# A full-array product ahead of each score tile in a two-layer transformer kernel

## What is computed

```python
x = x + _L0_xattn_ref(_layernorm(x), ctx_512, ...)   # 16 heads of 8: causal self attention + attention to ctx
x = x + _L0_ffn_ref(_layernorm(x), ...)              # 8 experts 128 -> 512 -> 128, weighted by the top 2
x = x + _L1_xattn_ref(_layernorm(x), ctx_512, ctx_512, ...)  # one head of 128
x = x + _L1_ffn_ref(_layernorm(x), ...)              # 16 heads of 64, values and outputs chosen by gates
...
att = jnp.where(causal, jnp.einsum('bhqd,bhkd->bhqk', q, k) * scale, -jnp.inf)
y = jnp.einsum('bhqk,bhkd->bhqd', jax.nn.softmax(att, axis=-1), v)
```

## Time and profile before

| | |
|---|---|
| median of 3 runs | 1716.87 us (1716.63 to 1721.53) |
| the profiled execution's own time | 1711.72 us |
| its span, first to last instruction | 1710.0 us |
| mean granted TensorE clock over the span | 0.718 of 2.4 GHz |
| TensorE busy | 1310.1 us (77%) |
| VectorE busy | 718.0 us (42%) |
| ScalarE busy | 488.1 us (29%) |

### The profile page before, as it was taken

How to read it: one execution, slowest core, us unless ns; L and a number is a source line. 1 busy time by engine, 2 the same in 40 slices (tenths; PEclk the granted TensorE clock), 3 DMA queues, 4 the chain that set the end, 5 groups by cost and what they waited for, 6 DMA issues and landing times.

```text
span 1710.0 us, 21323 instructions
## 1 busy us (share of the span) xinstructions
PE 1310.1 (77%) x8530; PEld 1008.1 (59%) x8530; DVE 718.0 (42%) x1958; ACT 488.1 (29%) x1003; POOL 77.1 (5%) x134
## 2 busy tenths in 40 slices
PE   2777668887679777896788777897688876897566
PEld 2446545775458654685457654596457754586366
DVE  2623492335822385225813376214832349122700
ACT  0233314224133232333143232333132231332120
POOL 0010001000010000100010000100010000100000
PEclk9657766787667875697658875697666976677655
DMA  5000010311012110301103110301103101121131
GB/s 157 7 1 4 0 31 4 64 44 26 12 28 43 38 28 10 64 19 28 34 1 64 44 29 10 58 13 41 25 10 64 44 16 22 26 41 38 37 59 46
DMA packets 197498, 56.85 MB, mean 33 GB/s; under 512 B 173029, under 2 KB 193303, under 8 KB 197399
## 3 DMA queue, kind: packets, MB, share of 16 engines
q1 hardware_dynamic: 195318, 51.30, 14.2%
q10 hardware_dynamic: 2080, 4.19, 0.8%
HBM read 31.36 MB, written 24.12 MB: 32 GB/s over the span
## 4 chain that ended last, share of the span: by engine, by line
PE 60%; DVE 23%; ACT 7%; issue 4%; DMA 3%; SPq 0%; ACTq 0%; DVEq 0%
PE bank L942 8%; PE bank L766 8%; PE bank L792 7%; DVE negmax L1179 6%; PE bank L692 6%; PE bank L904 4%; PE bank L618 4%; ACT pa L1012 3%; DVE negc L1331 3%; PE bank L925 3%; PE bank L707 2%; DVE qk_lo L1323 2%; DMA at<-at_d 2%; PE bank L956 2%; PE bank L717 2%
## 5 line engine op out<-in xcount | busy, mean ns | idle before, releaser
L1012 ACT ACTIVATE pa<-bank 128x512 f32<-128x512 f32 x224 | 123.4, 597 | 351.5 <-PE bank L707 266.2
L942 PE MATMUL bank<-vb,pb 128*128 128x65 f32 x1024 | 147.2, 315 | 12.2 <-issue 12.2
L942 PEld LDWEIGHTS bank<-vb,pb 128*128 128x128 f32 x1024 | 145.8, 232 | 16.4 <-issue 16.3
L766 PE MATMUL bank<-xnT_a,w 128*128 128x256 f32 x512 | 145.9, 436 | 0.0
L1179 DVE TENSOR_REDUCE negmax<-bank 128x2 f32<-128x512 f32 (+1 forms) x224 | 138.8, 682 | 16.2 <-PE bank L653 11.6
L1029 ACT ACTIVATE pa<-bank,b_c 128x256 f32<-128x256 f32 x256 | 107.3, 470 | 127.8 <-PE bank L766 126.4
L792 PEld LDWEIGHTS bank<-w,pa 128*128 128x128 f32 x1024 | 124.1, 193 | 3.0
L792 PE MATMUL bank<-w,pa 128*128 128x128 f32 x1024 | 124.1, 276 | 0.0
L766 PEld LDWEIGHTS bank<-xnT_a,w 128*128 128x128 f32 x512 | 106.7, 219 | 21.9 <-issue 7.0
L1087 ACT ACTIVATE pb<-bank 128x512 f32<-128x512 f32 x128 | 69.5, 595 | 169.7 <-PE bank L908 169.4
L692 PE MATMUL bank<-pa,va 128*32 128x256 f32 (+1 forms) x1024 | 101.8, 550 | 16.4 <-ACT pa L1012 15.9
(11 more groups left out here) (231 smaller groups left out, 1972.3 us busy)
## 6 DMA issues: line engine op xcount, KB each, us to landing
v_d<-vb SPq DMA_DIRECT2D x16, 512.0 KB, 5.1
vb<-v_d SPq DMA_DIRECT2D x16, 512.0 KB, 5.7
at_d<-at SPq DMA_DIRECT2D x32, 256.0 KB, 2.1
at<-at_d SPq DMA_DIRECT2D x32, 256.0 KB, 4.3
pv_d<-pvs SPq DMA_DIRECT2D x8, 512.0 KB, 2.8
pvs<-pv_d SPq DMA_DIRECT2D x16, 256.0 KB, 4.3
w<-in_L_ffn_W_dram ACTq DMA_DIRECT2D x1, 2048.0 KB, 10.4
bd<-mix_d SPq DMA_DIRECT2D x128, 8.0 KB
```

Source lines behind the costliest of these rows:

```text
L766: mm = pe.matmul(BA[u % 2][:, c * T:(c + 1) * T], w1[:, e, f:f + P], xnT_a[:, :], start=True, stop=True)
L942: mm = pe.matmul(BB[2 + qt][:, i * (DH + 1):(i + 1) * (DH + 1)], pb[:, h % NPB, kt * T + qt * P:kt * T + (qt + 1) * P], vb[:, kt, h, :], s ...
L1012: nc.scalar.activation(pa[:, e % NPA, :], BA[e % 2][:, :], ACT.Exp, scale=SC0).then_inc(S["a_ex"], 1)
```

## The change

A helper makes one product of the full array: `ident_b` (128x128 bf16) as weights and `mask_qk`, repeated four times, as 512 columns. It writes a whole bank. It is called after the wait for the bank and ahead of the bank's first score product, whose `start=True` lets the scores overwrite it. In `a_max` it is called for the four banks of blocks 1 to 6, in `a_score` for the two banks of pairs 1 to 13, in `b_max` for both banks of all eight blocks, in `b_score` for both banks of pairs 1 to 7.

```diff
+                    def full_array(bank):
+
+                        pe.matmul(bank[:, :].rearrange("p (n k) -> p n k", n=4), ident_b[:, :],
+                                  mask_qk[:, :].unsqueeze(1).broadcast_to([P, 4, P]), start=True, stop=True)
...
                                     if g == 0:
                                         pe.wait_ge(S["a_mx"], upto("a_mx", 4 * m - 3 + j))
+                                        full_array(BA[j])
                                     pe.matmul(BA[j][:, g * P:(g + 1) * P], qs[strips[j], sc, g, 0:P], ks[strips[j], sc, g, 0:P],
                                               start=(g == 0), stop=True, skip_group_check=True)
...
                                 if m > 0 and c == 0:
                                     pe.wait_ge(S["a_mx"], upto("a_mx", 4 * m - 3 + j))
+                                    full_array(BA[j])
...
                                     if n > 0 and kt == 0:
                                         pe.wait_ge(S["a_ex"], upto("a_ex", 2 * n - 1 + i))
+                                        full_array(BA[i])
...
                                     if c == 0:
                                         pe.wait_ge(S["a_ex"], upto("a_ex", 2 * n - 1 + i))
+                                        full_array(BA[i])
...
                                     if g == 0:
                                         pe.wait_ge(S["a_ex"], upto("a_ex", 2 * n - 1 + i))
+                                        full_array(BA[i])
...
                                 rows = slice(64 * j, 64 * j + 64)
+                                if c == 0:
+                                    full_array(BB[(2 * m + j + 2) % 4])
...
                                     if pr > 0 and kt == 0 and part == 0:
                                         pe.wait_ge(S["b_ex"], upto("b_ex", 2 * pr - 1 + i))
+                                        full_array(BB[i])
```

## The result

The changed kernel takes 1881.4 us (median of four runs, 1879.9 to 1898.4), the kernel before beside it 1719.1 (four runs): ratio 1.097, 95% interval 1.091 to 1.103, or +162 us. Forecast were 1949 us and +232, range 1770 to 2090. Some executions of a kernel are slower as a whole, at a lower granted clock: ratios and intervals leave them out, medians keep them.

The account below looks back on a forecast made before the run. It saw TensorE busy 77% of the span, mostly near half clock in partial-array stretches, with VectorE bounding the second maxima stretch. Seven periods at +27 (+189) plus ends +43 gave +232, 1949 us; range 1770 to 2090.

Parts of the forecast that it names:

- Price of one: Each added product in line, stream plus entering and leaving the strips: 0.94 us at half clock, 0.6 at full clock.
- Maxima, +13: Both attentions' maxima, per period: products in line, partly under VectorE's work, lengthen them by 13 us (4 to 26).
- First scores, +8: First attention's scores, per period: longer pairs, partly repaid by faster value products, +8 us (-1.5 to +21).
- I take six of these hot: First attention's scores: six of eight value-product heads per period reach full clock, 0.95 instead of 1.91 us each, -5.7 us.
- its clock 0.6 to 0.8: Sign of being right: the first-score stretch, 658 to 704, grows by some 8 us with its clock at this level.
- Second scores, +6: Second attention's scores beside the expert layers, per period: five pairs, two products each, +6 us (5 to 7).
- First period, +23 of the ends: First period, without second attention: six maxima blocks add 15 us and the scores 8.
- End, +20: End of the kernel, 1604 to 1704, at clock 0.50 throughout: score pairs add 14 us and maxima 6.
- seven score pairs x 2.1 = +14: End of the kernel: each of seven second-attention score pairs grows by 2.1 us at clock 0.50, +14 us.
- The clock wins all over: Rival: products raise the clock in maxima and scores and it holds; +8 us per period, 1783 us; chance 0.14.
- It never rises: Rival: the clock stays down, all products cost 0.94 us plus strips; 2148 us; chance 0.06.
- Faster: Rival: waits hide half the products, full clock in first scores takes off 14 us per period; 1673 us; chance 0.09.

Follow-up runs that it names:

- the winner: Two full-array products ahead of each first-attention score pair's wait (pairs 1 to 13), in a free bank, added to the kernel before, no others: 1664.4 us, ratio 0.973.

## Why the prediction was right, and where it was off

**Sign and mechanism: right.** Slower (0.88) came, inside the range; +162 against a forecast of +232 (0.70 of it; 0.80 by the profiled executions, 187). That the product costs more in line than its clock wins is shown by the runs: with the borders gathered the same 640 products cost +27, and 26 per sequence ahead of the wait turn the sign. The size is in part luck, since terms missed in both directions: the first scores more than forecast, the maxima, second scores and end less.

**Price of one.** Forecast 0.94 cold and 0.6 hot. Measured 1.05 - 0.21 = 0.84 cold: the borders are 0.41 together, not 0.51. They are counted from load to load here and from stream to stream in the forecast, so only the sum compares. At full clock, from the timeline of after:

```profile
1421.41 0.39 PE L598 MATMUL bank<-mask_qk,ident_b 128*128 128x512 bf16 x1 [0.78 <-ACT pa L1025]
...
1421.73 0.32 PE L736 MATMUL bank<-qs,ks 32*128 32x128 f32 x1
...
1421.98 0.39 PE L598 MATMUL bank<-mask_qk,ident_b 128*128 128x512 bf16 x1
```

0.32 + 0.25 = 0.57 for a product and a strip of 128 columns. The forecast took 0.11 us of stream for such a strip at half clock; half of it here is an estimate of 0.05, which leaves about 0.5 for the product. That the load isn't pulled across the border holds for product to strip: TensorE's loads stand 0.44 us at "issue" ahead of each strip's load, and that is gone where product and strip use the same rows. Had the load been pulled ahead, the sum would have been half, about +116; the measured +162 lies between the two, so the total does not decide it, and the rows at the border do. The rule stands in the Trainium skill ("TensorE: Matmul & The Clock Gate", Part 2, step 1) with two conditions that the prediction left out: the row groups don't conflict, or the load goes to the background weight buffer. Product and strip share rows, so the first is not met here. The rows above show no pull by the second either at a change of tile rows; without such a change the load comes 0.01 us after the product starts.

**Maxima, +13.** Measured +8.8 per sequence (61.6 / 7). Oversized, though the low end had been taken for its largest part; the clock over the stretch rose from 0.66 to 0.79. Which of its terms was too large no run parts. The terms price 36 of the 40 products: the block of maxima whose strips stand at 625.48 to 626.61 has none. TensorE idles 3.45 us before the next block, so its four may have been hidden.

**First scores, +8.** Measured +10.3 (72.1 / 7), but as a mix of +16 to +18 in three cold periods and +4 to +8 in the others. The pair was 2.86 us against 3.05 forecast. The step that failed is "I take six of these hot": in the cold periods no head gained. The value products of the six heads that lie in the stretch (busy PE and PEld, clock, DMA), in two periods of before and the same two of after:

```profile
659.70:697.60 37.90, 10.75 (x96) 3.65 (x96) 0.57 0.00 1
1248.70:1285.30 36.60, 9.36 (x96) 3.29 (x96) 0.64 0.00 1
```

```profile
737.90:792.10 54.20, 10.76 (x96) 3.57 (x96) 0.54 0.00 1
1404.80:1445.50 40.70, 7.41 (x96) 2.86 (x96) 0.83 0.00 1
```

10.76 us against 10.75 in the cold one, 7.41 against 9.36 in the hot one. Forecast were 5.7 us less in each period; over the seven periods these products took 68.7 us before and 63.8 after, 0.7 less in each. The period that the forecast was worked from, one of two alike (37.9 us at 0.57), had the slowest value products; four of the other five stood at 0.63 or 0.64. And "its clock 0.6 to 0.8" held in two periods of seven: three stood at 0.54, two at 0.83.

**Second scores, +6.** Measured +5.5 in the period that I had worked from, but +2.7 on the mean of seven, between the last exp of the first attention and the last addition of an expert's output (697.6 to 767.6 before, 792.1 to 867.6 after). Five of the seven periods had these layers at 0.84 to 0.88 before, and all have them at 0.93 or more after: there the clock gave a part back. The reading had a slip too: 704 to 766 hold six pairs, not five, and two of them (708.8, 713.7) are not at full clock, 1.6 us for twelve products instead of 0.91.

**First period, +23 of the ends.** Measured +23.8 (11.8 + 14.2 - 0.6 - 1.6). The maxima block was 1.88 longer, forecast 2.6; the scores there, at 0.50 throughout, cost more than forecast (14 against 8).

**End, +20.** Measured +7.8, the worst term: "seven score pairs x 2.1 = +14" was +4.3 in 1806.6 to 1863.7, and the rest +3.5. The border is not cheaper beside these 64-row strips: product and strip recur in 1.04 us here too (1816.90 to 1817.94). One cycle from exp to exp where the pair follows at once, before and after:

```profile
1637.52 1.08 ACT L1087 ACTIVATE pb<-bank 128x512 f32<-128x512 f32 x2 [0.74 <-PE bank L908]
1640.55 1.08 ACT L1087 ACTIVATE pb<-bank 128x512 f32<-128x512 f32 x2 [1.95 <-PE bank L908]
```

```profile
1820.39 1.08 ACT L1100 ACTIVATE pb<-bank 128x512 f32<-128x512 f32 x2 [2.32 <-PE bank L921]
1824.52 1.08 ACT L1100 ACTIVATE pb<-bank 128x512 f32<-128x512 f32 x2 [3.05 <-PE bank L921]
```

3.03 us became 4.13, +1.10 and not 2.1. It is the same +1.10 as in the first attention (1.76 to 2.86), where the forecast had +1.3: the second product stands partly where TensorE had waited for the second exp anyway (before, the second strip's load came 0.49 us after the first, released by that exp). Four of the seven pairs stand so, and together they make up the +4.3. The other three brought nothing on balance (-0.1 us), as two other things got shorter. The mixing of values takes 5.4 us instead of 7.4 at the slightly higher clock (0.53 against 0.50), and the attention over values waits less:

```profile
L942 PE MATMUL bank<-vb,pb 128*128 128x65 f32 x69 | 15.5, 420 | 11.1 <-issue 11.1
```

```profile
L955 PE MATMUL bank<-vb,pb 128*128 128x65 f32 x69 | 15.5, 419 | 8.7 <-issue 8.7
```

2.4 us of what the pairs lost had been slack. The forecast took the stretch as one that has no slack in it, from its clock alone, though the earlier trace rows have TensorE busy for only 65 of its 100 us.

By the profiled execution: seven sequences +155 (forecast 189), first period +24 (23), end +8 (20).

**The range.** The bounds given with the terms (4 to 26, -1.5 to +21, 5 to 7 per period, ends 10 to 60) add up to 1779 to 2155 us, wider than the "1830 to 2090 by its own bounds". The stated range was a judgement, and no sum gives it.

**Rivals.** The clock wins all over (1783) did not come; it did rise, but only part of the way (mean 0.718 to 0.756). It never rises (2148) is out by the hot periods. Faster needed 0.35 us or less in line per product; one in line was 0.84 or 0.5 in the change, and the winner shows what happens when it is near zero.

**What stays open.** Why the same scores stand at 0.54 in three consecutive periods and at 0.83 in later ones of the same execution; and which property of full-row products (the rows alone, the data moved, or the change of tile rows that comes with them) lifts the clock. Products over 32 rows and 32 columns together were not tried. With one product per pair the executions compared run from 1698 us at a mean clock of 0.732 to 1720 at 0.717, and no run shows what decides between them.

## What to carry to other kernels

Work added to lift TensorE's clock belongs ahead of a wait, where it fills idle time: 26 products per sequence are worth -47 us there, and +52 us behind the waits in alternation with strips. Don't alternate full-array products with partial-row tiles; gather them, since at half clock the two borders of a product (0.41 us) cost as much as its stream (0.43), and gathering alone took +162 us down to +27. Price such an edit by the pace of the engine that frees the buffers: in the first period's maxima a product and strip of 0.60 to 0.65 us, about one reduction (0.62), lengthened a block by 0.24 to 0.28 us, and one of 1.05 us by 1.88, since it falls behind at every bank. And don't let one period stand for all: of the seven later ones, the forecast's had the coldest scores (0.57) and the hottest expert layers (0.99).

## What was not expected of the hardware

A product over 32 of the 128 array columns, at 128 rows, lifts the clock as well as the full one (0.770 against 0.756 in the mean); one over 32 rows, at all columns, does not (0.63 against 0.95 in the same stretch). A full-array product with a stream of 32 columns pays both borders and leaves the clock of the scores at 0.50 to 0.56, lower than with no product at all (0.57 to 0.64). And the same stretch of program ran at two clocks within one execution, 54.2 us at 0.54 and 40.7 us at 0.83.
